# Handing one clear to ScalarE, starting unread matmuls one product earlier and rounding the fourth batch behind layer 1's first norm, in a two-layer gated cross-attention kernel

## The chip, the cores and the metric

The kernel runs on one core of a Trainium2 chip. The metric is the device time of one execution in microseconds (us), as the median of several runs.

## The reference, cut to what matters

x is 4 batches of 512 tokens with 128 features, the context 4 batches of 154 tokens. Two layers change x in place, each by a gated cross-attention (16 heads of 8) and a gated feed-forward part:

```python
x = x + tanh(g_xattn[0]) * L0_xattn(layernorm(x), ctx)
x = x + tanh(g_ffn[0])   * L0_ffn(layernorm(x))        # the quantised block
x = x + tanh(g_xattn[1]) * L1_xattn(layernorm(x), ctx)
x = x + tanh(g_ffn[1])   * L1_ffn(layernorm(x))

def L0_ffn(x):
    x = act_qdq(x)                        # 16 bits, scale = max |x| over ALL elements / 32767
    up = act_qdq(x @ dequant(w_up).T)     # 128 -> 384
    gate = act_qdq(x @ dequant(w_gate).T)
    gate = act_qdq(gate * fixed_u16(sigmoid(gate)))
    o = act_qdq(gate * up)
    return o @ dequant(w_down).T          # 384 -> 128
```

Each `act_qdq` needs a maximum over all four batches before any element can be rounded: five barriers in a row. The last of them, over gate times up, is called the product maximum here.

## The kernel before, in words

One program holds both layers. TensorE (PE), VectorE (DVE), ScalarE (ACT), GpSimd (POOL) and SyncE (SP, which issues the DMAs) each run their own list of instructions in the order in which it is written; semaphores tie the lists together. Features lie on the 128 partitions in the feed-forward part, one batch being 128x512, or 128x1536 for the 384 hidden features. In the attention stages a hand-written plan of slots sets the order; the quantised block in between is written out.

The end of the quantised block, where the change lies:

- DVE, `ffn()`: `outer(c)` multiplies gate and up magnitudes of batch c and keeps the maximum (L1470; signals `o_r`); `part_max(4, B)` reduces the four (L1403); `product16(1)` rounds a gate (L1465); `whole_top(4)` takes the maximum that PE spread over the partitions (L1411); `scale_of(4)` makes the scale (signals `sc_r`). Then `last16(c)` forms and rounds the product of batch c (L1476; signals `n3_r`), and for batch 0 DVE also scales it (L1534; `xod_r`). Behind `last16(2)` come `ffn_residual(0)` (L1482, waits for `down(0)`), `norm_stats("pre", 1, 0)` (L1293, L1296), `last16(3)`, `norm("pre", 1, 0)` (L1308) and `ffn_residual(1)`, then the statistics of batch 1, `ffn_residual(2)`, `q_low(1, 0)` and `ffn_residual(3)`.
- ACT: `up16(c)` and `product16(c)` round (L842, L854), the last being `up16(3)`; `product(1)`, `product(2)`, `product(3)` scale the products back (L858, waits for `n3_r`, signals `xo_r`); behind them `copy_normed("pre", 1, 0)` (L744) and `copy_q(1, 0)` (L751).
- PE: behind the third scale it waits for `o_r`, runs six unread products (`keep_warm`, L1102), `global_top(4)` (L1084), two and four more unread products, then `down(c)` for c = 0, 1, 2 (L1110, 12 products of 128x128 each, in two passes, so 24 rows), the transposes of `turn_normed("pre", 1, 0)` (L930), `project_q(1, 0)` (L936), `down(3)` and `turn_normed("pre", 1, 1)`.
- POOL: `clear_early` zeroes the query buffer Q4[1] (128x2048, L497), which layer 1's first batch uses; then `normed("pre", 1, 0)` makes 1/sqrt(var) (L626, L628) for DVE's norm, `normed("pre", 1, 1)` normalises batch 1, and `clear_late` zeroes further buffers behind `n3_r` and `xo_r`.
- SP: `queries(1, 0)` copies the query's high part twice and its low part once into Q4[1] (L434), and layer 1's first score matmul (`scores_for_top`, L953) waits for their landing. DVE reduces those scores (L1333).

Of the kernel before, what the change touches and what calls it, by code (L numbers as in the profile page):

```python
# [7 lines left out]
F32 = mybir.dt.float32  # L8
# [4 lines left out]
ACT = mybir.ActivationFunctionType  # L13
AX = mybir.AxisListType

P = 128
B, T, C = 4, 512, 128
TT = T // P
S = 154
H, D = 16, 8  # L20
G, J = 4, 4
# [180 lines left out]
def program(nc, x, w, wkr, ctxT, tailT, wffn, cols, rows, consts, masks, out):  # L202
    with ExitStack() as ctx:
# [33 lines left out]
        ones = sb("ones", [P, P])  # L237
# [119 lines left out]
        fmm, fev = sem("fmm"), sem("fev")  # L357
# [110 lines left out]
        def _(pool):  # L468
# [21 lines left out]
                pool.memset(Kd[2][:, :, :, :].bitcast(F32), 0.0).then_inc(kd_clear, 1)  # L490
                pool.memset(nil[:, :], 0.0).then_inc(nil_r, 1)

            def clear_early():

                pool.wait_ge(fmm, 24)
                pool.wait_ge(o_r, B)
                pool.memset(Q4[1][:, :, :].bitcast(F32), 0.0).then_inc(q4_clear, 1)  # L497

            def clear_late():

                pool.wait_ge(n3_r, B)
# [147 lines left out]
            for layer in range(2):  # L649
                normed("pre", layer, 0)  # L650
                if layer == 0:
                    pool.wait_ge(xn_r, 1)
                    pool.memset(Kd[1][:, :, :, :].bitcast(F32), 0.0).then_inc(kd_clear, 1)
                    pool.memset(V4[:, :, :, :, :], 0.0).then_inc(zero_r, 1)
                    pool.memset(VT[:, :, :, :], 0.0).then_inc(zero_r, 1)
                normed("pre", layer, 1)
                if layer == 0:
                    clear_rest()
                    normed("pre", 0, 2)
                    frames()  # L660
                    biases()
                    values(0)
                    q_low(0, 2)
                    tail_keys(0)
                else:
                    clear_late()
                for i in range(-1, B + 1):
                    masked = layer == 1 and 0 <= i < B
                    if i == -1 or 0 < i < B - 2:
                        b = max(i, 0) + 2  # L670
                        if i > 0:
                            normed("pre", layer, b)
                        if masked:
                            past(i, 0)
                        diagonal(layer, b)
                        if (layer, b) != (0, 2):
                            q_low(layer, b)
                    elif masked:
                        past(i, 0)
                    if masked:  # L680
                        past(i, 1)
                        past(i, 2)
                    if 0 <= i - 1 < B:
                        normed("post", layer, i - 1)
                    if masked:
                        past(i, 3)
                    if 0 <= i + 1 < B:
                        biased(layer, i + 1)
                if layer == 0:
                    pool.wait_ge(xq_r, B)  # L690
                    diagonal(1, 0)
                    values(1)
                    tail_keys(1)
                    clear_early()


        @block.scalar
        def _(act):
# [102 lines left out]
            for layer in range(2):  # L801
                for i in range(-1, B + 1):
                    for slot in range(SLOTS):
                        if 0 <= i < B and slot < TILES:
                            exps(layer, i, slot)
                        for what, b in planned(ACT_PLAN, layer, i, slot):
                            if what in ("pre", "post"):
                                copy_normed(what, layer, b)
                            elif what == "q":
                                copy_q(layer, b)  # L810
                            elif what == "top":
                                copy_top(layer, b)
                            else:
                                gate_of(b, int(what[4]))
                        if (layer, i) == (0, B):
                            for c in NEXT_KEYS_ACT.get(slot, ()):
                                copy_k(1, c)
                        if (layer, i, slot) in VALUES_AT:
                            copy_v(0, (VALUES_AT.index((layer, i, slot)),))
                        if (layer, i, slot) in WEIGHTS_AT:  # L820
                            k = WEIGHTS_AT[layer, i, slot]
                            n = min(4, 9 - 4 * k)
                            act.wait_ge(misc_full, use["w", k] + 1)
                            act.activation(wfT[:, 4 * k:4 * k + n, :], misc[:, 0:n * P], ACT.Copy).then_inc(wT_r, 1)
                if layer == 0:

                    def evacuate(t):
                        act.wait_ge(fmm, t + 1)
                        dst = gf if t < 12 else uf
                        act.activation(dst[:, t % 12 // 3, t % 3, :], fbank[t % FRING][:, :], ACT.Copy).then_inc(fev, 1)  # L830

                    def sigmoid16(c):
                        act.wait_ge(g16_r, c + 1)
                        act.wait_ge(sc_r, 2)
                        act.activation(gf[:, c, :, :], g16[:, c, :, :], ACT.Tanh, scale=sc[:, 1, 3:4]).then_inc(th_r, 1)
                        act.wait_ge(th_r, c + 1)
                        act.activation(s16[:, c, :, :], gf[:, c, :, :], ACT.Copy, bias=32768.0, scale=32768.0)\
                            .then_inc(s16_r, 1)

                    def up16(c):  # L840
                        act.wait_ge(sc_r, 3)
                        act.activation(u16[:, c, :, :], uf[:, c, :, :], ACT.Copy, scale=sc[:, 2, 2:3]).then_inc(u16_r, 1)  # L842

                    def up_size(c):
                        act.wait_ge(sc_r, 3)
                        act.activation(uabs[:, c, :, :], uf[:, c, :, :], ACT.Abs, scale=sc[:, 2, 2:3]).then_inc(uabs_r, 1)

                    def product_size(c):
                        act.wait_ge(sc_r, 4)
                        act.activation(n2abs[:, c, :, :], gf[:, c, :, :], ACT.Abs, scale=sc[:, 3, 3:4]).then_inc(n2abs_r, 1)  # L850

                    def product16(c):
                        act.wait_ge(sc_r, 4)
                        act.activation(g16[:, c, :, :], gf[:, c, :, :], ACT.Copy, scale=sc[:, 3, 3:4]).then_inc(n2a_r, 1)  # L854

                    def product(c):
                        act.wait_ge(n3_r, c + 1)
                        act.activation(gf[:, c, :, :], n2abs[:, c, :, :], ACT.Copy, scale=sc[:, 4, 1:2]).then_inc(xo_r, 1)  # L858

                    copy_v(1)  # L860
                    for c in range(1, B):
                        act.wait_ge(n16_r, c + 1)
                        act.activation(xq[:, c, :], n16[:, c, :], ACT.Copy, scale=sc[:, 0, 1:2]).then_inc(xq_r, 1)
                    for t in range(12):
                        evacuate(t)
                    evacuate(12)
                    sigmoid16(0)
                    evacuate(13)
                    sigmoid16(1)
                    for t in (14, 15):  # L870
                        evacuate(t)
                    sigmoid16(2)
                    for t in range(16, 24):
                        evacuate(t)
                    sigmoid16(3)
                    for c in range(B):
                        up_size(c)
                    for c in range(B):
                        product_size(c)
                    up16(0)  # L880
                    up16(1)
                    product16(2)
                    up16(2)
                    product16(3)
                    up16(3)
                    product(1)
                    product(2)
                    product(3)
                    copy_normed("pre", 1, 0)
                    copy_q(1, 0)  # L890
                    copy_normed("pre", 1, 1)
                    copy_q(1, 1)
                    diagonal(1, 1)
# [6 lines left out]
        def _(pe):  # L900
# [230 lines left out]
            for layer in range(2):  # L1131
# [46 lines left out]
                if layer == 0:  # L1178
# [20 lines left out]
                    for k in range(2, 4):  # L1199
                        global_top(k)  # L1200
                    pe.wait_ge(fev, 24)
                    pe.wait_ge(o_r, 2)
                    keep_warm(6)
                    global_top(4)
                    keep_warm(2)
# [19 lines left out]
        def _(dve):  # L1225
# [212 lines left out]
            def ffn():  # L1438
# [97 lines left out]
                last16(2)  # L1536
                ffn_residual(0)
                norm_stats("pre", 1, 0)
                last16(3)
                norm("pre", 1, 0)  # L1540
                ffn_residual(1)
                norm_stats("pre", 1, 1)
                ffn_residual(2)
                q_low(1, 0)
# [139 lines left out]
```

## Time and profile before

| | |
|---|---|
| median of 3 runs | 343.23 us (343.20 to 343.27) |
| span of the profiled execution, first to last instruction | 341.2 us |
| median less span | 2.0 us |
| PE busy | 279.0 us (82%) |
| DVE busy | 252.5 us (74%) |
| ACT busy | 192.6 us (56%) |
| POOL busy | 136.7 us (40%) |
| mean granted TensorE clock | 0.957 |

The page gives the profiled execution by its span alone; the 2.0 us around it are the difference to the median. "Busy" is the time in which an engine has an instruction at work. Times of rows count from the first instruction of the span. A row of the timeline merges instructions of one kind that follow each other; its first number is the start, the second the time from the first one's start to the last one's end.

### The profile page before, as it was taken

How to read it: one execution, taken by the hardware profiler on the slowest of the kernel's cores; microseconds unless marked ns; L12 is line 12 of the kernel's file. 1: busy time of each engine (PE TensorE's matmuls, PEld its weight loads, DVE VectorE, ACT ScalarE, POOL GpSimd, SP SyncE). 2: the span in 40 equal slices, each digit the busy share in tenths (PEclk: the TensorE clock that was granted, in tenths of full speed). 3: DMA queues.
4: the chain of work that ended last, by engine and by line, in shares of the span. 5: the costliest groups of instructions: out<-in, count | busy, mean ns of one | idle time of the engine just before them, and what ended most of it. 6: DMA issues, size and time to landing. Idle time of an engine off the chain costs nothing. (4 is left out here: it accounts for less than half of the span.)

```text
span 341.2 us, 4468 instructions
## 1 busy us (share of the span) xinstructions
PE 279.0 (82%) x1424; PEld 160.7 (47%) x1424; DVE 252.5 (74%) x538; ACT 192.6 (56%) x303; POOL 136.7 (40%) x274
## 2 busy tenths in 40 slices
PE   0889899899989779985007888899998998999994
PEld 0558544455434345331005776664654654444462
DVE  5699875877996388889989977986596693441834
ACT  1673367556476746779589632446656446665232
POOL 6669893750050411870002059921386207131100
PEclk9999999999999999997556999999999999999998
DMA  7930100010000000000000002220001000000004
GB/s 204 336 146 3 69 32 10 27 73 10 1 8 3 0 0 2 1 0 0 1 0 0 2 0 92 94 100 2 10 25 76 8 0 10 1 0 3 0 1 123
DMA packets 9687, 12.55 MB, mean 37 GB/s; under 512 B 896, under 2 KB 5376, under 8 KB 9664
## 3 DMA queue, kind: packets, MB, share of 16 engines
q1 hardware_dynamic: 9232, 11.80, 9.7%
q10 hardware_dynamic: 432, 0.47, 0.7%
q8 instruction: 11, 0.18, 0.2%
q14 instruction: 12, 0.10, 0.1%
HBM read 4.27 MB, written 1.05 MB: 16 GB/s over the span
## 5 line engine op out<-in xcount | busy, mean ns | idle before, releaser
L1333 DVE TENSOR_REDUCE sb_nm<-ps_top 128x3 f32<-128x462 f32 (+2 forms) x168 | 96.0, 626 | 26.6 <-PE ps_top L953 13.9
L772 ACT ACTIVATE sb_pr<-ps_score 128x512 f32<-128x512 f32 (+1 forms) x148 | 82.3, 583 | 58.8 <-PE ps_score L985 49.2
L953 PE MATMUL ps_top<-sb_Kd,sb_Q 128*128 128x462 f32 (+3 forms) x240 | 69.7, 349 | 4.7 <-DVE sb_nm L1333 2.4
L985 PE MATMUL ps_score<-sb_Q,sb_Kd 128*128 128x512 f32 x119 | 54.4, 467 | 1.3 <-ACT sb_pr L772 1.0
L953 PEld LDWEIGHTS ps_top<-sb_Kd,sb_Q 128*128 128x128 f32 x240 | 42.6, 188 | 18.1 <-DVE sb_nm L1333 11.9
L626 POOL TENSOR_SCALAR sb_var<-sb_mv 128x4 f32<-128x4 f32 x16 | 4.7, 291 | 83.3 <-DVE sb_mv L1296 82.9
L985 PEld LDWEIGHTS ps_score<-sb_Q,sb_Kd 128*128 128x128 f32 x119 | 22.2, 188 | 31.6 <-ACT sb_pr L772 23.4
L1017 PE MATMUL ps_pv<-sb_pr,sb_V 128*32 128x512 f32 x256 | 34.1, 605 | 0.0
L620 POOL TENSOR_SCALAR_AFFINE_SELECT sb_pr<-sb_pr 128x512 f32<-128x512 f32 x16 | 10.6, 661 | 46.4 <-ACT sb_pr L772 46.4
L1353 DVE STREAM_TRANSPOSE sb_oq<-ps_pv 128x512 f32<-128x512 f32 x16 | 10.8, 700 | 12.4 <-PE ps_pv L1017 12.3
L643 POOL TENSOR_SCALAR sb_xn<-sb_xr,sb_nmean,sb_rstd 128x128 f32<-128x128 f32 x44 | 19.3, 453 | 1.2
L628 POOL TENSOR_TENSOR sb_rstd<-sb_var,sb_half 128x4 f32<-128x4 f32 x16 | 17.7, 1106 | 1.3
L521 POOL CAST sb_Kd<-sb_K 32x616 fp32r<-32x616 f32 x20 | 14.1, 703 | 8.5 <-DVE sb_K L1244 7.4
L1017 PE MATMUL ps_pv<-sb_pr,sb_VT 128*32 128x512 f32 (+1 forms) x128 | 14.9, 550 | 0.9 <-ACT sb_pr L772 0.9
L1102 PE MATMUL ps_top<-sb_wfT 128*128 128x256 f32 x30 | 9.5, 472 | 7.2 <-DVE sb_amax L1470 6.4
L991 PE MATMUL ps_score<-sb_Q,sb_KT 128*128 128x384 f32 (+1 forms) x29 | 12.9, 454 | 2.7 <-ACT sb_pr L772 2.7
L1293 DVE BATCH_NORM_STATS2 sb_stat<-sb_xr 128x6 f32<-128x128 f32 x64 | 13.9, 280 | 1.4 <-DMA sb_xr<-x 1.2
L497 POOL MEMSET sb_Q<- 128x2048 f32 x1 | 1.8, 1804 | 32.6 <-DVE sb_amax L1470 32.6
L930 PE MATMUL ps_misc<-sb_consts,sb_xn 128*128 128x128 f32 x64 | 10.4, 287 | 5.1 <-POOL sb_xn L643 2.3
L1195 PE MATMUL ps_top<-sb_front,sb_wfT 128*128 128x512 f32 x22 | 12.1, 682 | 2.7 <-ACT sb_uf L830 2.2
L1084 PE MATMUL ps_misc<-sb_consts,sb_amx 128*128 128x128 f32 x8 | 2.5, 400 | 14.2 <-DVE sb_amx L1403 14.2
L604 POOL TENSOR_TENSOR sb_xg<-sb_xr,sb_bog 128x128 f32<-128x128 f32 x32 | 13.6, 457 | 0.1
(180 smaller groups left out, 556.5 us busy)
## 6 DMA issues: line engine op xcount, KB each, us to landing
sb_Q<-sb_qh SPq DMA_DIRECT2D x16, 256.0 KB, 2.3
sb_Q<-sb_ql SPq DMA_DIRECT2D x8, 256.0 KB, 3.3
sb_xr<-x SPq DMA_DIRECT2D x4, 256.0 KB, 7.7
out<-sb_xr SPq DMA_DIRECT2D x4, 256.0 KB, 2.5
sb_wsb<-w SPq DMA_DIRECT2D x1, 704.0 KB, 9.0
sb_wf<-wffn SPq DMA_DIRECT2D x1, 576.0 KB, 8.6
sb_wkr<-wkr SPq DMA_DIRECT2D x2, 256.0 KB, 7.1
sb_Q<-sb_nmT SPq DMA_DIRECT2D x16, 32.0 KB
```

Of the source, the lines that this page charges most:

```text
L521: ins = pool.tensor_copy(Kd[n % 3][q, :, j, :], K4[q, :, b, :])
L604: ins = pool.tensor_tensor(xg[:, n % 2, t, :], xr[:, TT * b + t, :], bog[:, layer, :], ALU.add)
L628: pool.tensor_tensor(rstd[:, k % 4, :], var[:, k % 4, :], half[:, :], ALU.pow).then_inc(rstd_r, 1)
L643: ins = pool.tensor_scalar(xn[:, kind == "post", t, :], xr[:, TT * b + t, :], nmean[:, k % 4, t:t + 1], rstd[:, k % 4, t:t + 1], ALU.add, ...
L772: act.activation(pr[:, k % PRING, q0:T], score_bank(B * layer + b, t)[:, q0:T], ACT.Exp, scale=SCALE).then_inc(exp_r, 1)
L953: ins = pe.matmul(cols[:, c0:c1, :], Q4[n % 3][:, g, P * qt:P * qt + P], Kd[n % 3][:, g, j:j + c1 - c0, 0:keys], start=True, stop=not mask ...
L985: ins = pe.matmul(ps[:, :], Kd[n % 3][:, g, j, 0:P], Q4[n % 3][:, g, :], start=True, stop=True, skip_group_check=True)
L991: ins = pe.matmul(ps[:, q0:T], KT[:, b, t - H, :], Q4[n % 3][:, t - H, q0:T], start=True, stop=(layer == 0), skip_group_check=True)
L1017: ins = pe.matmul(acc[32 * g:32 * g + 32, q0:T], lhs, pr[:, (TILES * n + t) % PRING, q0:T], start=(r in (0, 2)), stop=(r >= 4), skip_group ...
L1195: pe.matmul(fbank[t % FRING][:, :], wfT[:, 3 * (t // 12) + m, :], xq[:, c, :], start=True, stop=True).then_inc(fmm, 1)
L1293: ins = dve.bn_stats(stat6[:, k % 4, t, :], xr[:, TT * b + t, :])
L1333: dve.tensor_reduce(nm[:, :, :].rearrange("p t h -> p (t h)")[:, f0:f0 + heads], top[k % MRING][:, 0:keys * heads].rearrange("p (h k) -> p ...
```

## The change

Four edits in the end of the quantised block. POOL's clear of Q4[1] goes, and ScalarE writes the same zeros instead, with an activation that multiplies a broadcast 128x128 tile of ones by 0.0, between `up16(3)` and `product(1)`; it waits for all four `outer`. PE's wait ahead of the six unread products is for the first `outer` and no longer for the second. On DVE `ffn_residual(1)` and `norm("pre", 1, 0)` now stand ahead of `last16(3)`.

```diff
-            def clear_early():
-
-                pool.wait_ge(fmm, 24)
-                pool.wait_ge(o_r, B)
-                pool.memset(Q4[1][:, :, :].bitcast(F32), 0.0).then_inc(q4_clear, 1)
-
...
                     tail_keys(1)
-                    clear_early()
...
+                    def clear_query():
+
+                        act.wait_ge(o_r, B)
+                        act.activation(Q4[1][:, :, :].rearrange("p g (t c) -> p (g t) c", c=P),
+                                       ones[:, :].unsqueeze(1).to_broadcast([P, G * TT, P]), ACT.Copy, scale=0.0)\
+                            .then_inc(q4_clear, 1)
+
...
                     up16(3)
+                    clear_query()
                     product(1)
                     product(2)
                     product(3)
...
                     pe.wait_ge(fev, 24)
-                    pe.wait_ge(o_r, 2)
+                    pe.wait_ge(o_r, 1)
                     keep_warm(6)
                     global_top(4)
...
                 ffn_residual(0)
                 norm_stats("pre", 1, 0)
+                ffn_residual(1)
+                norm("pre", 1, 0)
                 last16(3)
-                norm("pre", 1, 0)
-                ffn_residual(1)
                 norm_stats("pre", 1, 1)
```

## Rows read from the trace of the kernel before

**Rows 1.** Stretches of time: length, busy PE, PEld, DVE, ACT, POOL, PEclk, DMA, GB/s

```profile
154.80:158.10 3.30, 3.30 (x4) 0.79 (x3) 3.30 (x3) 3.27 (x4) 0.00 (x0) 0.50 0.00 0
...
161.70:185.40 23.70, 5.94 (x14) 4.54 (x15) 21.98 (x34) 18.79 (x14) 0.99 (x1) 0.50 0.00 0
185.50:207.00 21.50, 17.31 (x123) 14.75 (x121) 18.00 (x39) 11.38 (x10) 7.72 (x11) 1.00 0.10 37
```

**Rows 2.** Timeline of DVE to the fourth scale and behind it

```profile
175.71 1.02 DVE L1465 TENSOR_SCALAR sb_g<-sb_gf,sb_sc 128x1536 int16<-128x1536 f32 x1
...
179.15 0.08 DVE L1470 DVE_READ_ACCUMULATOR2_ANT sb_amax<- 128x1 f32 x1
...
184.30 0.16 DVE L1403 TENSOR_REDUCE sb_amx<-sb_amax 128x1 f32<-128x4 f32 x1
184.37 2.65 DVE L1465 TENSOR_SCALAR sb_g<-sb_gf,sb_sc 128x1536 int16<-128x1536 f32 x1
186.95 0.27 DVE L1411 TENSOR_REDUCE sb_sc<-ps_misc 128x1 f32<-128x128 f32 x1
...
187.95 1.82 DVE L1476 SCALAR_TENSOR_TENSOR sb_s<-sb_g,sb_sc,sb_u 128x1536 int16<-128x1536 int16 x1
...
190.74 3.54 DVE L1476 SCALAR_TENSOR_TENSOR sb_s<-sb_g,sb_sc,sb_u 128x1536 int16<-128x1536 int16 x2
```

**Rows 3.** Timeline of PE in the same stretch, weight loads left out

```profile
181.05 5.02 PE L1102 MATMUL ps_top<-sb_wfT 128*128 128x256 f32 x12 [6.41 <-DVE sb_amax L1470]
185.91 0.38 PE L1084 MATMUL ps_misc<-sb_consts,sb_amx 128*128 128x128 f32 x2
...
190.88 2.94 PE L1110 MATMUL ps_score<-sb_wfT,sb_gf 128*128 128x128 f32 x24 [0.91 <-DVE sb_gf L1534]
194.22 2.94 PE L1110 MATMUL ps_score<-sb_wfT,sb_gf 128*128 128x128 f32 x24 [0.39 <-ACT sb_gf L858]
```

**Rows 4.** Timeline of ACT behind its last rounding

```profile
188.92 1.56 ACT L842 ACTIVATE sb_u<-sb_uf,sb_sc 128x1536 int16<-128x1536 f32 x1
192.59 1.57 ACT L858 ACTIVATE sb_gf<-sb_s,sb_sc 128x1536 f32<-128x1536 int16 x1 [2.11 <-DVE sb_s L1476]
...
198.00 1.58 ACT L858 ACTIVATE sb_gf<-sb_s,sb_sc 128x1536 f32<-128x1536 int16 x1 [2.11 <-DVE sb_s L1476]
201.09 0.60 ACT L744 ACTIVATE sb_xnT<-ps_misc 128x512 f32<-128x512 f32 x1 [1.51 <-PE ps_misc L930]
```

**Rows 5.** Timeline of DVE behind last16(2), to layer 1's first norm

```profile
194.20 0.75 DVE L1482 SCALAR_TENSOR_TENSOR sb_xr<-ps_score,sb_tg,sb_xr 128x512 f32<-128x512 f32 x1
...
196.18 1.79 DVE L1476 SCALAR_TENSOR_TENSOR sb_s<-sb_g,sb_sc,sb_u 128x1536 int16<-128x1536 int16 x1
199.23 1.11 DVE L1308 TENSOR_SCALAR sb_xn<-sb_xr,sb_mv,sb_rstd 128x128 f32<-128x128 f32 x4 [1.26 <-issue]
200.26 0.74 DVE L1482 SCALAR_TENSOR_TENSOR sb_xr<-ps_score,sb_tg,sb_xr 128x512 f32<-128x512 f32 x1
```

**Rows 6.** Timeline: PE's query product, SP's DMAs, layer 1's first score product

```profile
201.84 1.10 PE L936 MATMUL ps_misc<-sb_xnT,sb_wsb 128*128 128x512 f32 x2 [0.78 <-ACT sb_xnT L744]
...
203.74 1.23 SPq L434 DMA_DIRECT2D sb_Q<-sb_qh  x2
...
207.46 0.48 PE L953 MATMUL ps_top<-sb_Kd,sb_Q 128*128 128x512 f32 x1 [0.89 <-issue]
```

**Rows 7.** Timeline of POOL: its clear, and the variance of layer 1's first norm

```profile
184.41 1.80 POOL L497 MEMSET sb_Q<- 128x2048 f32 x1 [32.60 <-DVE sb_amax L1470]
...
196.36 1.67 POOL L626 TENSOR_SCALAR sb_var<-sb_mv 128x4 f32<-128x4 f32 x1 [10.15 <-DVE sb_mv L1296]
```

**Rows 8.** Single lines of ACT: durations in ns (min/median/max), first and last start

```profile
L837 ACT ACTIVATE sb_s<-sb_gf x4: 1483/1483/1483, 149.1 to 163.4; 128x1536 uint16<-128x1536 f32 x4
...
L830 ACT ACTIVATE sb_gf<-ps_top x5: 578/597/598, 135.0 to 140.8; 128x512 f32<-128x512 f32 x5
```

**Rows 9.** Timeline of PE around the granted clock's first fall

```profile
151.33 1.02 PE L1195 MATMUL ps_top<-sb_front,sb_wfT 128*128 128x512 f32 x2
154.57 3.62 PE L1195 MATMUL ps_top<-sb_front,sb_wfT 128*128 128x512 f32 x4 [2.22 <-ACT sb_uf L830]
```

## The prediction

> **What bounds the kernel now.** The page first: no engine is busy all through, so a share of busy time prices nothing here. I then read stretches [rows 1], the timelines of the single engines around the edits [rows 2 to 5, 7] and what starts layer 1 [rows 6]. In the stretches the reader sees the quantised block at the low level of TensorE's clock (granted 0.50, which is 1.2 GHz), its end at the full level (1.00, 2.4 GHz), and DVE the busiest engine in both. In the timelines one path can be followed. DVE takes the spread maximum at 186.95 and rounds products at 187.95 and from 190.74 [rows 2]; ACT scales batch 1 from 192.59 [rows 4]; PE's `down(1)` starts at 194.22 [rows 3]; DVE adds the first residual at 194.20, rounds batch 3 at 196.18 and normalises at 199.23 [rows 5]; ACT copies the transposed norm at 201.09 [rows 4]; PE projects it at 201.84, SP issues the query's DMAs at 203.74, and the first score product of layer 1 runs at 207.46 [rows 6]. From there on layer 1 follows. So the change is read off at one point: the start of ACT's copy, 201.09 now. By how much that moves, the end moves, unless something later takes it up.
>
> **The part that brings time.** POOL's clear (1.80) begins at 184.41 [rows 7], within 0.04 of DVE's `product16(1)`, which takes 2.65 where the same form took 1.02 without company [rows 2]. With the clear gone I take 1.02, so DVE is free at 184.37 + 1.02 = 185.4 and not 187.0. For the spread maximum to be there, PE has to be early too. Its six unread products ran from 181.05 and let `global_top(4)` start at 185.91, 4.86 later, while the reduced maximum was ready at 184.46 [rows 2, 3]. On the first `outer`, whose accumulator is read at 179.15 to 179.23 [rows 2], they begin at about 179.4 and are through by 184.3; the maximum at 184.46 ends last, and the spread one is there at about 185.3. Both edits are needed and give the same point: the read at 186.95 moves to about 185.35, by 1.6. Everything on DVE down to `last16(2)` is 1.6 earlier: batch 1 is rounded at 192.5 - 1.6 = 190.9, batch 2 at 194.27 - 1.6 = 192.7. `down(0)` starts at 189.3.
>
> **The part that takes it back: the clear on ACT.** ACT runs without a gap up to `up16(3)`, started at 188.92 [rows 4], and none of that depends on the product maximum, so it doesn't move. Each such instruction starts 1.47 behind the one before (1.56 less an overlap of 0.09), so the clear starts at 190.39 (its wait, for all four `outer`, ended at 184.3; behind it in ACT's list stand the three `product` and the copy). No row shows it. The nearest are the ones without a scale tile: 1.483 at 1536 columns, 0.597 at 512 [rows 8], a slope of 0.865 ns per column, so 2048 take 1.483 + 0.443 = 1.92. Bounds: from below 1.36, were it as fast per column as DVE's fast form (1.02 for 1536 [rows 2]); from above 2.40, four times the 512 row. I take 1.92, the line through the two nearest rows. `product(1)` then starts at 190.39 + 1.92 - 0.09 = 192.22, although its data is there at 190.9. Against 192.59 [rows 4] only 0.37 of the 1.6 is left.
>
> The Trainium skill (ScalarE: Activation LUTs, section on what ACT_TABLE_LOAD costs) gives 186 ns plus 0.833 ns per column for an activation with immediate operands, an estimate of 1.89 here. By it the copy would come 0.03 earlier than in the sum below. No row of this case shows a 2048-column activation.
>
> **The part that costs: the new order on DVE.** `down(1)` starts 0.37 earlier, at 193.85, and takes 2.94 [rows 3]; `ffn_residual(1)` starts at 196.83, and DVE idles for about two microseconds ahead of it, as statistics of batch 0 are done by 194.7. It takes 0.75, the norm starts at 197.6 and gives way after 1.03 (199.23 to 200.26 [rows 5]), so `last16(3)` starts at 198.64, where it stood at 196.18. ACT's `product(3)` followed it by 1.82 (196.18 to 198.00 [rows 4, 5]): 200.46. And here is the queue: `copy_normed` stands behind `product(3)` in ACT's list. It can start 1.49 later, at 201.95. The transposes it copies are ready long before: the norm ends at 198.7, PE finishes `down(2)` at about 199.5 and turns it by 200.15. So the copy waits 1.8 for its own queue, and starts at 201.95 instead of 201.09: **0.86 later**.
>
> Small things. POOL's variance step took 1.67 under `last16(3)` [rows 7]; that cover is gone, it is short now, but the norm waits for the residual and not for it, so it brings nothing. Behind the copy, all steps keep their distance: projection 202.7, DMAs 204.6, first score product 208.3. `down(3)` is started behind the projection and ends at about 206.5, `turn_normed("pre", 1, 1)` by 207.2, before the scores. POOL's later clears wait for `product(3)`, done at 202.0, while POOL is with batch 1's norm until about 205; nothing queues there. SP has no DMA in between. The unread products count for nothing themselves: PE waits at that point.
>
> **Sum.** Gain upstream 1.6, of which ACT's clear leaves 0.37; the order adds 1.23 to it (copy at 201.95): net +0.86. The profiled execution spans 341.2, 2.0 less than the median of 343.23; I leave those 2.0 alone. Forecast 343.23 + 0.86 = 344.1. With the clear at 1.36 the net is +0.30 (343.5), at 2.40 it is +1.34 (344.6).
>
> **Rivals.**
> - *The clock falls.* In the new order PE idles from about 200.15 to 202.7, 2.5 us. The granted clock fell to 0.50 in this kernel right behind an idle 2.22 of PE, short work before it [rows 1, 9]. If it falls before the projection, that doubles: four such rows took 3.62 at 1.2 GHz [rows 9], so two 1.8 to 1.9 instead of 1.10 [rows 6], and the rest of `down(3)` is slow too. Price 0.4 to 0.8: 344.5 to 344.9. For it: the longest idle of PE in this stretch so far is 0.9 [rows 3, 6]. Against it: `down(1)` and `down(2)` run 5.6 without a gap before. Chance 0.25.
> - *A later stage takes it up.* If the first score product waits for something else than the query's landing, or DVE's idle half microseconds behind it absorb the shift, the end moves less: 343.3 to 343.8. Against it: DVE's reductions follow the scores, and the page names nothing else that ends near 207.4. Chance 0.15.
> - *Not slower: the clear isn't in the way.* Place: ACT between `up16(3)` and `product(1)`. If the activation takes under 1.06 the copy is no later than now; at 0.65 or less `product(1)` starts with its data at 190.9, `down(1)` at 192.6 and the copy at about 200.7, 0.4 earlier: 342.8. To be faster by more than 0.2% a further 0.3 would have to come from POOL, which is done earlier with batch 1 and disturbs DVE less. Against it: ACT's own rows, none of which is under 0.96 ns per column [rows 8]. Chance 0.12.
> - *The change doesn't do what it says.* If `product16(1)` stays at 2.65, the scale isn't earlier; ACT ends the clear at 192.3 all the same, so the loss is as forecast. This rival moves the reasons, not the time; it lies in the forecast's chance, 0.48.
>
> **How the numbers follow.** About 0.2% (0.69 us) is what a measurement of this kernel can tell from no change. The forecast's case holds +0.30 to +1.34 around +0.86; about 0.39 of its 0.48 is over 0.69, 0.09 inside. The clock's case is slower altogether, 0.25. The absorbing case is inside 0.2% for 0.10, slower for 0.05. The short clear is inside for 0.04, faster for 0.08. Sum: slower 0.69, same 0.23, faster 0.08. The range reaches from 342.8, the end of the short clear, to 345.1, the clock's case with the clear a little above my price.
>
> **What would show it.** Right: `product16(1)` near 1.0; the spread maximum read near 185.35; the clear on ACT from 190.4 for 1.9; `product(1)` right behind it, near 192.2; DVE idle for 2 us before `ffn_residual(1)`; `product(3)` near 200.5 and ACT's copy right behind it, near 201.95, with no wait for PE; PE idle 2.5 us before the projection, at a granted clock of 1.00. Wrong: a copy released by PE's transposes, ahead of 201; a clear much shorter or longer than 1.9; a granted clock of 0.50 after 202; or a copy late by 0.9 with layer 1's end less late.

## The result, and the profile after

| | before | changed |
|---|---|---|
| median | 343.25 us (20 runs, 342.54 to 344.37) | 344.29 us (20 runs, 343.10 to 345.70) |
| ratio | | 1.0029, 95% interval 1.0019 to 1.0039 |
| span of the profiled execution | 341.2 us | 342.5 us (its own time 344.43) |

The change costs 1.04 us by the medians. The forecast was 344.1, and its chain of steps can be laid over the new trace. "The copy" is always ACT's copy of the transposed norm, and "the query's copy" the one behind the projection. Line numbers past 700 differ a little between the kernels. The timeline of DVE, in the changed kernel, against [rows 2, 5]:

```profile
184.21 0.16 DVE L1404 TENSOR_REDUCE sb_amx<-sb_amax 128x1 f32<-128x4 f32 x1
184.28 1.01 DVE L1466 TENSOR_SCALAR sb_g<-sb_gf,sb_sc 128x1536 int16<-128x1536 f32 x1
185.25 0.29 DVE L1412 TENSOR_REDUCE sb_sc<-ps_misc 128x1 f32<-128x128 f32 x1
...
189.06 3.54 DVE L1477 SCALAR_TENSOR_TENSOR sb_s<-sb_g,sb_sc,sb_u 128x1536 int16<-128x1536 int16 x2
...
196.70 0.75 DVE L1483 SCALAR_TENSOR_TENSOR sb_xr<-ps_score,sb_tg,sb_xr 128x512 f32<-128x512 f32 x1 [2.11 <-PE ps_score L1111]
197.36 1.11 DVE L1309 TENSOR_SCALAR sb_xn<-sb_xr,sb_mv,sb_rstd 128x128 f32<-128x128 f32 x4
198.38 1.81 DVE L1477 SCALAR_TENSOR_TENSOR sb_s<-sb_g,sb_sc,sb_u 128x1536 int16<-128x1536 int16 x1
```

The reader sees the gain and where it goes. Without POOL beside it `product16(1)` takes 1.01 instead of 2.65, and the spread maximum is read at 185.25 instead of 186.95. But DVE then stands idle for 2.11, waiting for `down(1)`, before the residual of batch 1, and `last16(3)` starts at 198.38 where it was at 196.18. The timeline of ACT, against [rows 4]:

```profile
188.83 1.56 ACT L835 ACTIVATE sb_u<-sb_uf,sb_sc 128x1536 int16<-128x1536 f32 x1
190.30 1.90 ACT L856 ACTIVATE sb_Q<-sb_ones 128x2048 fp32r<-128x2048 f32 x1
192.10 3.03 ACT L851 ACTIVATE sb_gf<-sb_s,sb_sc 128x1536 f32<-128x1536 int16 x2
200.23 1.58 ACT L851 ACTIVATE sb_gf<-sb_s,sb_sc 128x1536 f32<-128x1536 int16 x1 [5.11 <-DVE sb_s L1477]
201.72 0.58 ACT L737 ACTIVATE sb_xnT<-ps_misc 128x512 f32<-128x512 f32 x1
204.52 0.69 ACT L744 ACTIVATE sb_qh<-ps_misc,sb_cols 128x512 fp32r<-128x512 f32 x1 [2.23 <-PE ps_misc L937]
```

The clear takes 1.90 and `product(1)` follows it at once. `product(3)` waits 5.11 for `last16(3)`, and the copy has no wait of its own: it follows `product(3)`. The timeline of PE (weight loads left out), against [rows 3, 6]:

```profile
179.28 5.46 PE L1103 MATMUL ps_top<-sb_wfT 128*128 128x256 f32 x12 [4.73 <-DVE sb_amax L1471]
184.53 0.68 PE L1085 MATMUL ps_misc<-sb_consts,sb_amx 128*128 128x128 f32 x2
...
193.71 2.94 PE L1111 MATMUL ps_score<-sb_wfT,sb_gf 128*128 128x128 f32 x24 [1.56 <-ACT sb_gf L851]
...
199.18 0.60 PE L931 MATMUL ps_misc<-sb_consts,sb_xn 128*128 128x128 f32 x4
202.44 2.04 PE L937 MATMUL ps_misc<-sb_xnT,sb_wsb 128*128 128x512 f32 x2 [2.66 <-ACT sb_xnT L737]
...
209.00 0.48 PE L954 MATMUL ps_top<-sb_Kd,sb_Q 128*128 128x512 f32 x1 [0.73 <-DVE sb_xr L1483]
```

The transposes are done at 199.8, and PE idles 2.66. Then the projection takes 2.04 instead of 1.10. The stretches of the changed kernel say why (columns as in [rows 1]): the granted clock fell to its low level, 1.2 GHz, behind that idle. The forecast had named "a granted clock of 0.50 after 202" as a sign that it is wrong, and here it is.

```profile
185.50:202.40 16.90, 11.67 (x88) 10.26 (x86) 14.15 (x32) 11.69 (x9) 2.05 (x4) 1.00 0.00 1
202.60:205.80 3.20, 3.20 (x10) 2.17 (x11) 0.56 (x1) 0.69 (x1) 3.01 (x7) 0.51 0.00 0
206.00:212.00 6.00, 5.27 (x35) 4.17 (x33) 4.10 (x13) 0.60 (x1) 4.58 (x6) 1.00 0.34 131
```

Executions differ by several tenths of a microsecond already ahead of the changed part, so profiles are best laid over each other at one event. I take the start of the reduce of the four product maxima (184.30 before [rows 2], 184.21 after) as zero, and subtract it from starts in the timelines and from the span. "DVE's split" is where DVE parts the maxima of layer 1's first scores into a high and a low part, which SP's next DMA carries on:

| us behind that reduce | copy | query's copy | first score product | DVE's split of the maxima | their DMA | end of the span |
|---|---|---|---|---|---|---|
| before | 16.79 | 18.67 | 23.16 | 36.62 | 39.03 | 156.91 |
| changed | 17.51 | 20.31 | 24.79 | 38.26 | 40.33 | 158.25 |
| difference | +0.72 | +1.64 | +1.63 | +1.64 | +1.30 | +1.34 |

Three terms come out: +0.72 up to the copy, +0.92 in the projection, and -0.34 between DVE's split and the DMA. From there to the end only 0.04 is added. The experiments take them one by one.

### The profile page after: what moved, and what is told of

Same layout as the page of the kernel before. It is cut to its first block and busy times, and to the rows that moved or that the text cites. A ratio compares the mean times of both kernels' runs of the same rounds, so it can differ in the third digit from the quotient of the medians.

```text
span 342.5 us, 4468 instructions
## 1 busy us (share of the span) xinstructions
PE 282.8 (83%) x1424; PEld 163.3 (48%) x1424; DVE 250.4 (73%) x538; ACT 194.3 (57%) x304; POOL 133.6 (39%) x273
## 5 line engine op out<-in xcount | busy, mean ns | idle before, releaser
L620 POOL TENSOR_SCALAR sb_var<-sb_mv 128x4 f32<-128x4 f32 x16 | 3.2, 200 | 119.1 <-DVE sb_mv L1297 118.6
L912 PE MATMUL ps_score<-sb_ctx,sb_wkr 128*128 128x308 f32 x16 | 6.1, 514 | 8.4 <-DMA sb_wkr<-wkr 8.4
L958 PE MATMUL ps_top<-sb_maskr,sb_identr 128*128 128x512 f32 (+3 forms) x48 | 12.8, 267 | 0.0
```

## The experiments

Three causes had to be told apart: the copy's place behind `product(3)` (the queue), the clear, and the clock. All runs below are compared with the kernel before on the same chip; its medians were 343.26 for the first four, 343.08 for the next four and 343.22 for the last two.

**The old order of DVE in the changed kernel.**

```diff
-                ffn_residual(1)
-                norm("pre", 1, 0)
                 last16(3)
+                norm("pre", 1, 0)
+                ffn_residual(1)
```

> The changed kernel with DVE's order of before: last16(3), then the norm, then the residual of batch 1. Queue theory (ScalarE's copy waits behind product(3), which waits for last16(3), which the new order puts behind down(1)): last16(3) starts near 194.5, product(3) follows product(2) at once, near 196.4, and no longer holds the copy; the norm starts near 197.5, PE turns it behind down(2) near 199.3, the copy starts near 199.9, so 1.2 us ahead of the kernel before: 342.0, 2.2 us less than the changed kernel. Rival (the clear on ScalarE is the whole cost, the order does nothing): the copy stays within 0.3 of the changed kernel's 201.7 and the time at 344.0 to 344.4. Rival (what was lost is only the fall of TensorE's clock ahead of the projection): idle of PE is gone here as well, so about 0.8 less than the changed kernel, 343.5.

Measured: 341.44, ratio 0.9946 (0.9932 to 0.9960), faster than both kernels. The rows are of ACT and of DVE:

```profile
196.21 1.58 ACT L851 ACTIVATE sb_gf<-sb_s,sb_sc 128x1536 f32<-128x1536 int16 x1 [1.21 <-DVE sb_s L1477]
199.69 0.60 ACT L737 ACTIVATE sb_xnT<-ps_misc 128x512 f32<-128x512 f32 x1 [1.90 <-PE ps_misc L931]
```

```profile
194.39 1.79 DVE L1477 SCALAR_TENSOR_TENSOR sb_s<-sb_g,sb_sc,sb_u 128x1536 int16<-128x1536 int16 x1
197.43 1.11 DVE L1309 TENSOR_SCALAR sb_xn<-sb_xr,sb_mv,sb_rstd 128x128 f32<-128x128 f32 x4 [1.25 <-issue]
```

The copy now waits for PE and not for its own queue, and starts at 15.60 behind the reduce, 1.91 earlier than in the changed kernel. The norm itself starts 13.34 behind the reduce, against 13.15 in the changed kernel: all that the new order gave it is 0.19. PE's idle ahead of the projection is 0.78 here and the projection takes 1.10, so the clock didn't fall either: the 2.85 between the two medians are 1.91 at the copy and about 0.94 of the clock, as measured below.

**The new order alone, in the kernel before.** POOL clears, PE waits for the second `outer`.

```diff
+                ffn_residual(1)
+                norm("pre", 1, 0)
                 last16(3)
-                norm("pre", 1, 0)
-                ffn_residual(1)
```

> The kernel before with nothing but DVE's new order: POOL still zeroes the buffer, PE still waits for the second product. Queue theory: down(1) as before from 194.2, residual of batch 1 at 197.2, norm near 197.9, last16(3) near 199.0, product(3) near 200.8, copy near 202.3 against 201.1, so +1.2 in the copy, and a little more if TensorE's clock falls in the longer idle: 344.4 to 345.2. Rival (the order does nothing or helps, because the norm comes earlier): 343.0 to 343.3.

Measured: 344.62, ratio 1.0042 (1.0025 to 1.0058). ACT's timeline:

```profile
200.57 1.57 ACT L858 ACTIVATE sb_gf<-sb_s,sb_sc 128x1536 f32<-128x1536 int16 x1 [4.84 <-DVE sb_s L1476]
202.05 0.58 ACT L744 ACTIVATE sb_xnT<-ps_misc 128x512 f32<-128x512 f32 x1
```

The copy is at 17.92, 1.13 later than before, and follows `product(3)` without a wait. So the order alone makes a loss, and a bit more than the whole change. It does so by both ways: PE idled 2.66 here too, and the clock fell behind it, as the projection shows, which began at full clock and took 1.67 where it takes 1.10 otherwise.

```profile
202.77 1.67 PE L936 MATMUL ps_misc<-sb_xnT,sb_wsb 128*128 128x512 f32 x2 [2.66 <-ACT sb_xnT L744]
```

**The copy ahead of `product(3)`, in the changed kernel.** It keeps a wait for `last16(3)`, over whose data it writes.

```diff
+                    act.wait_ge(n3_r, B)
+                    copy_normed("pre", 1, 0)
                     product(3)
-                    copy_normed("pre", 1, 0)
```

> The changed kernel with one swap in ScalarE's list: the copy of the transposed norm stands ahead of product(3); it waits for last16(3), since its target lies over the data which that reads. Queue theory: the copy starts at the end of last16(3), near 200.2 instead of 201.7, product(3) behind it near 200.8, the copy of the query near 202.3 instead of 204.5; 342.4 to 343.0. Rival (the copy waits for PE's transposes or DVE, not for its queue): copy at 201.7 and time as the changed kernel, 344.2.

Measured: 342.39, ratio 0.9974 (0.9964 to 0.9984). ACT's timeline:

```profile
200.40 0.60 ACT L737 ACTIVATE sb_xnT<-ps_misc 128x512 f32<-128x512 f32 x1 [5.11 <-DVE sb_s L1478]
200.89 1.57 ACT L851 ACTIVATE sb_gf<-sb_s,sb_sc 128x1536 f32<-128x1536 int16 x1
202.36 0.68 ACT L744 ACTIVATE sb_qh<-ps_misc,sb_cols 128x512 fp32r<-128x512 f32 x1
```

With DVE's new order untouched, two lines of ACT's list turn the loss into a gain. The copy starts 16.01 behind the reduce, 1.50 earlier than in the changed kernel, although `product(3)`'s data is there no sooner. That is the queue theory's sharpest test, and it holds: the copy was held by what stood in front of it. Not all of the gain of 1.90 in the medians is the queue's: PE's idle is 1.20 here, and the projection took 1.10.

**The clear behind `product(2)`, in the changed kernel.**

```diff
-                    clear_query()
                     product(1)
                     product(2)
+                    clear_query()
```

> The changed kernel with the clear behind product(2) instead of ahead of product(1), in ScalarE's idle time. Theory (the clear ate 1.2 of the 1.6 us gained upstream): product(1) starts near 190.9 instead of 192.1, down(1) near 192.5 instead of 193.7, residual of batch 1 near 195.5, last16(3) near 197.2, the copy near 200.5: 1.2 us less than the changed kernel, 343.0 with the clock as it is there. Rival (the clear is hidden and its place is free): product(1) later for another reason, time unchanged at 344.2.

Measured: 342.73, ratio 0.9987 (0.9974 to 1.0001). ACT's timeline:

```profile
191.30 1.58 ACT L851 ACTIVATE sb_gf<-sb_s,sb_sc 128x1536 f32<-128x1536 int16 x1 [0.48 <-DVE sb_s L1477]
...
194.51 1.89 ACT L856 ACTIVATE sb_Q<-sb_ones 128x2048 fp32r<-128x2048 f32 x1
199.45 1.57 ACT L851 ACTIVATE sb_gf<-sb_s,sb_sc 128x1536 f32<-128x1536 int16 x1 [3.04 <-DVE sb_s L1477]
200.93 0.58 ACT L737 ACTIVATE sb_xnT<-ps_misc 128x512 f32<-128x512 f32 x1
```

The copy is at 16.29 behind the reduce, 1.22 earlier than in the changed kernel: that is what the clear's place ate. In this profile PE idled 2.66 as well, yet the projection took 1.10: the clock did not fall. So of the 1.56 in the medians the profile shows 1.22 from the place, and the rest can be the clock, in a part of the executions. Against the kernel before the run isn't told apart (its interval reaches 1.0001).

**PE waiting for the second `outer` again, in the changed kernel.**

```diff
-                    pe.wait_ge(o_r, 1)
+                    pe.wait_ge(o_r, 2)
```

> The changed kernel with PE waiting for the second outer again, as before the change. Theory (in the changed kernel the earlier scale is covered by the clear): the spread maximum is read near 186.5 instead of 185.3, product 1 rounded near 192.0, still ahead of the clear's end at 192.1, so everything from product(1) on stays: 344.2, no difference from the changed kernel. Rival (the earlier scale reaches the copy): 1.1 us slower, 345.3.

Measured: 344.29, ratio 1.0039 (1.0026 to 1.0052), the changed kernel's own median. DVE and ACT:

```profile
186.40 0.29 DVE L1412 TENSOR_REDUCE sb_sc<-ps_misc 128x1 f32<-128x128 f32 x1 [1.30 <-PE ps_misc L1085]
```

```profile
190.10 1.89 ACT L856 ACTIVATE sb_Q<-sb_ones 128x2048 fp32r<-128x2048 f32 x1
192.06 1.57 ACT L851 ACTIVATE sb_gf<-sb_s,sb_sc 128x1536 f32<-128x1536 int16 x1
```

Behind the reduce the maximum is read 1.34 later, and still `product(1)` starts 0.07 behind the clear's end, and the copy only 0.16 later than in the changed kernel. As long as the clear stands there, the edit on PE is worth less than the medians can tell. PE's row ahead of the query's copy shows that the clock fell behind 2.66 of idle in this profile too:

```profile
202.41 1.48 PE L937 MATMUL ps_misc<-sb_xnT,sb_wsb 128*128 128x512 f32 x2 [2.66 <-ACT sb_xnT L737]
```

**Unread products in PE's idle, in the changed kernel.**

```diff
                     turn_normed("pre", 1, 0)
+                    keep_warm(4)
                     project_q(1, 0)
```

> The changed kernel with four more unread products on PE between the transposes of the first norm and the query's projection, where it idles 2.7 us. Theory (part of the loss is TensorE's clock, which falls in that idle in a part of the executions): the granted clock stays at 1.00 through the projection, which takes 1.1 instead of 2.0; the copy stays near 201.7; the median falls by 0.5 to 0.8, to 343.5, and the spread of the runs narrows. Rival (the clock's fall is hidden behind the DMAs or down(3)): 344.2, no difference. By the forecast's own sum without a fall the time is 344.1.

Measured: 343.44, ratio 1.0015 (1.0005 to 1.0026). PE's timeline, and the stretch that was at the low clock:

```profile
199.76 1.89 PE L1103 MATMUL ps_top<-sb_wfT 128*128 128x256 f32 x8
202.59 1.10 PE L937 MATMUL ps_misc<-sb_xnT,sb_wsb 128*128 128x512 f32 x2 [0.93 <-ACT sb_xnT L737]
```

```profile
202.60:205.80 3.20, 3.20 (x23) 2.72 (x24) 0.75 (x1) 0.69 (x1) 3.01 (x7) 1.00 0.02 6
```

The copy is at 17.51 as in the changed kernel, to the hundredth; the projection takes 1.10, the query's copy comes at 19.36 instead of 20.31. The clock's price is 0.95 in the profile. In the medians it is 0.85, both against the changed kernel and against the run just above, which was on the same chip; by the ratios to the kernel before it is 0.5 against the changed kernel and 0.8 against the run above. The profiles agree closely on it, if one takes the time from the copy's start to the start of DVE's split:

| profile | PE idle ahead of the projection | projection | from the copy to the split |
|---|---|---|---|
| before | 0.78 | 1.10 | 19.83 |
| changed | 2.66 | 2.04 | 20.75 |
| order alone | 2.66 | 1.67 | 20.73 |
| second `outer` | 2.66 | 1.48 | 20.71 |
| clear behind `product(2)` | 2.66 | 1.10 | 19.79 |
| unread products | 0.93 | 1.10 | 19.79 |

So behind an idle of 2.66 the clock fell in three of four profiled executions. It fell at the projection's start in one and within it in two, and cost 0.92 to 0.96 by the split in all three. What it didn't take from the projection it took from `down(3)` behind it (3.55, 3.96 and 4.15 where it is 2.84 at full clock), whose residual DVE adds before it reduces the first scores.

With the fall gone the change still costs 0.36 by the two medians (the ratio's interval is 0.17 to 0.9), and the profile's end lies 0.34 behind that of before: +0.68 at the first score product, -0.34 at the split. In how many executions of the changed kernel the clock fell at this place isn't shown. The 7 of 20 with a mean granted clock of 0.964 or 0.965 have a median of 343.62 and the other 13 of 344.43, but that mean counts every stretch: of 61 runs of the kernel before, which has no such idle, the 7 at 0.952 have a median of 344.31.

**Both repairs**, the old order and the later clear.

```diff
-                    clear_query()
                     product(1)
                     product(2)
+                    clear_query()
...
-                ffn_residual(1)
-                norm("pre", 1, 0)
                 last16(3)
+                norm("pre", 1, 0)
+                ffn_residual(1)
```

> The changed kernel with both repairs: DVE's order of before, and the clear behind product(2). Theory: product(1) near 190.9, last16(3) from 194.4, the clear on ScalarE from 194.2 to 196.1 and product(3) at 196.2 at once. The norm waits for POOL's variance step, which meets last16(3) again, so near 197.4 as in the run with the old order alone; but down(2) is over near 198.1 instead of 199.0, so PE turns at 198.5 and the copy starts near 199.2, half a microsecond earlier than there: 341.0. Rival (the copy is set by the norm chain already with the old order alone): 341.4, no difference.

Measured: 341.45, ratio 0.9957 (0.9945 to 0.9969). The expected half microsecond over the old order alone didn't come. The copy did start earlier, at 15.16 against 15.60, and the first score product at 21.51 against 21.94. But the DMA of the maxima is at 37.38 against 37.47, and the end at 155.23 against 155.36: 0.34 is lost in the same step in which the changed kernel had won 0.34.

**Both repairs, PE waiting for the second `outer`.**

```diff
-                    pe.wait_ge(o_r, 1)
+                    pe.wait_ge(o_r, 2)
```

> The kernel with both repairs, but PE waiting for the second outer as before the change. Theory (with the clear out of the way the earlier scale is worth its time): the maximum read near 186.5 instead of 185.3, product(1) near 192.0, the copy near 200.3 instead of 199.2: 1.1 us slower than the kernel with both repairs, 342.1. Rival (the first edit brings nothing, since PE or POOL set the pace): 341.0, no difference.

Measured: 342.62, ratio 0.9986 (0.9973 to 0.9999), 1.17 above the median with both repairs. DVE and ACT:

```profile
187.00 0.29 DVE L1412 TENSOR_REDUCE sb_sc<-ps_misc 128x1 f32<-128x128 f32 x1 [1.34 <-PE ps_misc L1085]
```

```profile
192.66 1.57 ACT L851 ACTIVATE sb_gf<-sb_s,sb_sc 128x1536 f32<-128x1536 int16 x1 [1.91 <-DVE sb_s L1477]
```

The copy is at 16.59 behind the reduce, 1.43 later than with both repairs, where 1.1 was expected. The same edit of one number that moved next to nothing in the changed kernel is worth a microsecond in the medians once ACT waits for data there again. How much depends on the clock: the twelve runs have medians of 341.59 at a mean granted clock of 0.962 (three), 342.54 at 0.958 (three) and 343.11 at 0.953 (six), and the profile is one of the last. Its stretch from 185.5 to 187.0 still has a clock of 0.65, where the one with both repairs has 1.00. Taking the clear off POOL brings little by itself: with PE's wait as before, the copy of this profile is only 0.20 earlier than in the kernel before, though its later clock has a part in that. PE's edit with POOL's clear in place was not run.

**POOL's subtraction behind DVE's split, in the kernel with both repairs.** This is for the 0.34. The rows before and after are DVE's split (a cast and a subtraction, 128x64) and POOL's low part of the third query, first in the kernel before, then in the changed one:

```profile
220.92 0.66 DVE L1344 CAST sb_nms<-sb_nm 128x64 fp32r<-128x64 f32 x1
...
220.25 1.26 POOL L614 TENSOR_TENSOR sb_ql<-sb_qf,sb_qh 128x512 fp32r<-128x512 f32 x1
```

```profile
222.47 0.33 DVE L1345 CAST sb_nms<-sb_nm 128x64 fp32r<-128x64 f32 x1
...
221.45 1.27 POOL L608 TENSOR_TENSOR sb_ql<-sb_qf,sb_qh 128x512 fp32r<-128x512 f32 x1 [1.16 <-ACT sb_qf L748]
```

The cast's length is the whole term: from its start to the DMA it is 2.41 before and 2.07 in the changed kernel. Before, POOL comes to the subtraction straight from its diagonal copies and starts 0.67 ahead of the cast. In the changed kernel POOL is through with those sooner relative to the query and waits for ACT, so it starts 1.02 ahead, and the cast meets only its end.

```diff
+                if (layer, b) == (1, 2):
+                    pool.wait_ge(nms_r, B + 1)
                 pool.tensor_tensor(ql[...], qf[...], qh[...], ALU.subtract)
```

> The kernel with both repairs, and POOL's low part of layer 1's third query waits until DVE has split the score maxima of layer 1's first batch. Contention theory (0.34 us of any shift ahead of this point was taken up or given away because DVE's split of the maxima, 128x64, met POOL's subtraction of 128x512 at a different point: 0.66 for the cast where POOL began just before it, 0.33 where it began a microsecond before): the cast takes 0.23 and the subtraction 0.28, as elsewhere in the layer, so the maxima's DMA comes 0.5 us sooner behind the cast's start than the 2.4 of the kernel with both repairs: 340.9 to 341.0. Rival (the step from the split to the DMA is long for another reason, PE or the copy): 341.4, cast as before.

> The kernel with both repairs once more, on the same chip as the one with POOL's wait, to have the pair side by side. By the theory of the contention it gives 341.4 to 341.5 again, 0.5 more than its neighbour; by the rival both are the same.

Measured: 340.78, ratio 0.9926 (0.9913 to 0.9940), and 341.77, ratio 0.9951 (0.9937 to 0.9964), for its twin without the wait. DVE and POOL with the wait:

```profile
219.34 0.22 DVE L1347 CAST sb_nms<-sb_nm 128x64 fp32r<-128x64 f32 x1
219.59 0.26 DVE L1349 TENSOR_TENSOR sb_nms<-sb_nm,sb_nms 128x64 fp32r<-128x64 f32 x1
```

```profile
220.11 1.28 POOL L610 TENSOR_TENSOR sb_ql<-sb_qf,sb_qh 128x512 fp32r<-128x512 f32 x1 [1.56 <-DVE sb_nms L1349]
```

From the cast's start to SP's DMA (221.16) it is 1.82, in the twin 2.38 (219.08 to 221.46): 0.56 less, as expected. The medians differ by 0.99 in five runs each; the profiles bear out only 0.56, with the ends of the span, behind the reduce, 0.52 apart. This is the fastest version found, 2.4 us below the kernel before.

## Why the prediction was right

By its own steps:

- *POOL's clear and the wait on PE bring 1.6 at the scale.* 1.01 for `product16(1)` (1.02 taken), the read at 185.25 (185.35). Right. That PE's edit doesn't reach the copy behind the clear is shown by the run with the second `outer`, and that POOL's is worth only 0.20 without it by the run with both repairs and the second `outer`.
- *The clear costs 1.92 and leaves 0.37.* It took 1.90. `product(1)` started at 192.10; behind the reduce that is 0.40 ahead of before. Right. The estimate from the Trainium skill (ScalarE: Activation LUTs, What ACT_TABLE_LOAD costs) was 1.89, and the trace agrees.
- *`ffn_residual(1)` waits, `last16(3)` slides, `product(3)` holds the copy.* Every row of this chain was there, and three experiments test it (the old order, the order alone, the copy ahead). The size was 0.86 and measured 0.72. Most of the difference is the residual ahead of the norm: priced as 0.77 from one start to the next, it took 0.66 (196.70 to 197.36).
- *Behind the copy all steps keep their distance.* This step failed, twice, in opposite directions. The clock fell in the profiled execution, +0.92 at the query's copy; the rival had its mechanism right and its price a little low (0.4 to 0.8, measured 0.92 to 0.96), and its chance of 0.25 looks too low, as the clock fell in three of the four profiles with that idle. And 0.34 was taken up at DVE's split, where the rival of the absorbing stage looked at idle time and not at contention: its place was wrong, its size right (it left the end 0.1 to 0.6 late, and without the fall the profile's end is 0.34 late).

So 344.1 against 344.29 is a meeting of errors: 0.72 + 0.92 - 0.34 = 1.30 stands in the profile where 0.86 was forecast, and the medians, in which the fall need not be in every execution, give 1.04. What the forecast's own case, without a fall, is worth was measured by itself: 0.34 in the profile and 0.36 in the medians, where 0.86 was forecast (the interval of the medians, 0.17 to 0.9, holds both; the terms of the profile, about 0.7 up to the first score product less 0.34 at the split, say which). The direction, the place and the queue are right by the mechanism; that the time met the forecast to 0.2 is in part luck, and the 0.36 without the fall lie inside the 0.2% that the prediction took for no change.

## What to carry to other kernels

Before an instruction is put later on one engine, follow its consumer into the consumer's own list: here it was not `last16(3)` that anyone waited for, but the copy behind `product(3)`. An operation moved to another engine costs by its place in that list, and the free place was two instructions further on. An edit that measures as nothing can be worth a microsecond once the one that covers it has moved, so test edits of a bundle one by one and in pairs. And where a forecast is met, lay its steps over the trace all the same: here errors of 0.92 and 0.34 stood behind the copy, in opposite directions.

## What the runs showed of the hardware that was not expected

- Behind the same idle of 2.66 us PE's granted clock fell in three profiled executions (the changed kernel, the order alone, the second `outer`) and stayed at 1.00 in the one with the clear moved. Where it fell, the projection's two rows of 512 columns took 2.04, 1.67 and 1.48 instead of 1.10, and the way from the copy to the split 0.92 to 0.96 more in each.
- A DVE cast of 64 columns took 0.22 alone, 0.33 and 0.66 beside a POOL subtraction of 512 columns, 0.66 where POOL had begun 0.67 before it and still had 0.6 to go. In both the cast ended just behind the subtraction, by 0.07 and 0.08. The Trainium skill (GPSIMD Engine Reference, Specifications) names this: the two share their SBUF interfaces, and DVE instructions in a two-port mode or with two SBUF inputs contend. The trace agrees that they contend, for `product16(1)` (2.65 against 1.01) and for the cast, which have one SBUF input each; in which mode they ran no run here shows. It shows the other direction too: POOL's variance step of 4 columns took 1.67 beside DVE's `last16(3)`, which has two SBUF inputs, and 0.20 without it.

```profile
194.76 0.20 POOL L620 TENSOR_SCALAR sb_var<-sb_mv 128x4 f32<-128x4 f32 x1 [43.05 <-DVE sb_mv L1297]
```

(That row is of the changed kernel's POOL, against [rows 7].)
